# Moving the feed-forward evacuation of ScalarE, VectorE and GpSimd one piece later, behind the next attention step

## The chip, the core and the metric

The kernel runs on one core of a Trainium2 chip. The core has five engines that run side by side, each through its own list of instructions in order, and wait for one another by semaphores: TensorE (PE: matmuls; its weight loads are PEld), VectorE (DVE), ScalarE (ACT), GpSimd (POOL) and SyncE (SP, which here only starts DMAs). The metric is the device time of one execution in microseconds, lower is better. The chip grants TensorE one of two clocks, 1.2 or 2.4 GHz; the profile shows it as 0.50 and 1.00.

## The reference

Input x is 8 sequences of 512 tokens of 256 features, all float32. Four blocks are applied, each on a layernorm of x and added to x:

```python
x = x + ssm(layernorm(x))       # projection, rotary state space scan of 8 heads, gate, rms norm, projection
x = x + ffn(layernorm(x))
x = x + deltanet(layernorm(x))  # q, k, v, beta; delta-rule scan of 8 heads of 32; layernorm
x = x + ffn(layernorm(x))       # the same weights as above

def ffn(x):                     # ternary weights w, a scale s for each output feature
    h = silu(x @ w1.T * w1_s) * (x @ w2.T * w2_s)      # 256 -> 1024
    h = gelu(h @ h1.T * h1_s)                          # 1024 -> 1024
    h = gelu(h @ h2.T * h2_s)                          # 1024 -> 1024
    return h @ w3.T * w3_s                             # 1024 -> 256
```

## The kernel before, in words

A **stage** is the work of one attention block on one sequence: the state space block (`ssm_stage`, four tiles of 128 tokens, eight steps each) or the delta rule (`delta_stage`, 89 steps: 20 of projections and Gram matrices, 31 of a triangular inverse on VectorE, then the recurrence in blocks of 32 tokens). Beside each stage but the very first state space one, `window` runs the feed-forward block of another sequence (`ffn`). So there are 7 state space windows and 8 delta-rule windows, and one feed-forward block alone at the end.

The feed-forward block works on two units of 256 tokens. A unit is 18 **slices**, numbered s: 8 for w1/w2 (called w0 to w7 here, 8 matmuls each), 4 for h1 (h1.0 to h1.3, 32 matmuls), 4 for h2, one for the transposes of the next unit's input (xt) and one for w3 (32 matmuls). Each float32 operand is split in a high and a low part, so that matmuls come in pairs with `_hi` and `_lo`. A slice writes one of four PSUM banks, in a ring: `bank` makes slice s wait until slice s-4 has been read.

What the other engines do for a slice is its **evacuation**. For w slices: silu on ScalarE into `gate` (L698), the product on VectorE into `hid` (L899, which frees the bank, L902), the high part on VectorE (L903), the low part on GpSimd (L580). For h slices: two gelus on ScalarE (L702, L703), the high part (L706), the low part on GpSimd (L580). `hid` and `gate` have two buffers, so ScalarE's slice n waits for the low part of slice n-2 (L695). For w3: scale and residual on VectorE (L922, L925).

The order on every engine is written by the same function. A list (`SSM_PLAN`, `DELTA_PLAN`, made by `spread`) gives each attention step a number of slices; `window` (L129) emits attention step i, then all feed-forward pieces whose position lies below the sum of the plan up to i. A w slice and xt are one piece at position s; an h slice and w3 are two, at s and s + 0.5: for an h slice the first piece is 12 matmuls (input tiles k = 0 to 5 for the first half of the outputs), the second the other 20, of which the last 8 use k = 6 and 7. Each piece of TensorE waits for the low parts that it reads: slice h1.0 reads w0 to w7 (k = 0 to 7), and slice h2.0 reads h1.3 in its last 8 matmuls (L1215). The evacuation stands at s + 0.5, so it is emitted in the attention step in which TensorE's last piece of the slice is.

In a state space window a unit spans two tiles (a pair). TensorE's order around the places that matter is, for the first tile: projections (L1261), w1 to w5; cumulative sums (L1269 to L1281), w6, w7, h1.0 and 12 matmuls of h1.1; transposes L1290. For the second tile: transposes L1251, the end of h1.3; projections (L1261), h2.0; sums (L1269 to L1281), h2.1, h2.2; transposes L1290. ScalarE's part behind L1261 is softplus, two copies, silu and a copy (L722 to L730), for which it waits for VectorE's L942, which waits for L1261. VectorE's part behind the sums is a chain of 15 operations from L952 to L976, with sine and cosine on ScalarE in between.

## Time and profile before

| | |
|---|---|
| median of 3 runs | 3181.72 us (3176.04 to 3186.53) |
| the profiled execution | 3179.42 us, its span 3177.4 us, mean granted clock 0.891 |
| busy share of the span | PE 78%, PEld 69%, DVE 47%, ACT 36%, POOL 29% |
| chain that ended last, by engine | PE 46%, DVE 25%, ACT 10%, issue 10%, POOL 5%, DMA 3% |

The time of the runs and of the profiled execution differ by 2.3 us in the median. TensorE is the busiest engine, but it is idle for 686 us of the span, and a part of its busy time runs at the lower clock. So what counts is what TensorE waits for at each place of the order, and at which clock it goes on.

### The profile page before, as it was taken

To read this page: it belongs to the slowest core of one execution; us is meant where nothing else is said; L and a number is where in the kernel's file an instruction comes from. 1 tells how busy PE (TensorE), PEld (TensorE's weight loads), DVE (VectorE), ACT (ScalarE), POOL (GpSimd) and SP (SyncE) were. 2 spreads that over 40 slices of the span, in tenths; PEclk is the share of its full clock that TensorE was granted. 3 is DMA by queue.
4 is the path that set the end of the run, shared out by engine and by line. 5 is a ranking of instruction groups with operands and counts; after the bars stand their busy time and mean duration, and the time that the engine had idled before them with its cause. 6 is when DMAs were issued, how large, how long until landed. Compare 5 with 4: busy or idle time off the path is not lost.

```text
span 3177.4 us, 54420 instructions
## 1 busy us (share of the span) xinstructions
PE 2491.4 (78%) x20928; PEld 2195.7 (69%) x20928; DVE 1483.2 (47%) x3604; ACT 1157.8 (36%) x2426; POOL 926.0 (29%) x1216
## 2 busy tenths in 40 slices
PE   4678868888688886888868888678877888777688
PEld 3567757777577775787657776568766777666578
DVE  3434553445534445444454444545444444544541
ACT  2235432445225442245412544134432354323223
POOL 2123323233223232233323223232322233233233
PEclk7679988999799997999979998789987999898799
DMA  6000000000000000000000000000000000000000
GB/s 202 1 1 1 3 12 15 1 1 18 19 7 1 1 18 21 4 1 1 20 21 3 1 8 21 14 1 1 15 14 14 1 1 10 12 15 6 21 10 7
DMA packets 86976, 43.33 MB, mean 14 GB/s; under 512 B 71472, under 2 KB 81584, under 8 KB 86704
## 3 DMA queue, kind: packets, MB, share of 16 engines
q1 hardware_dynamic: 83040, 28.12, 3.5%
q0 software_dynamic: 3664, 11.53, 1.1%
q8 instruction: 177, 2.90, 0.4%
q14 instruction: 95, 0.78, 0.1%
HBM read 27.05 MB, written 12.58 MB: 12 GB/s over the span
## 4 chain that ended last, share of the span: by engine, by line
PE 46%; DVE 25%; ACT 10%; issue 10%; POOL 5%; DMA 3%; SPq 1%; DVEq 0%; POOLq 0%; ACTq 0%
PE F L1218 21%; DVE prod L1079 4%; DVE ti L1081 3%; PE Q L1261 3%; PE F L1240 2%; PE Q L1329 2%; PE Q L1346 2%; PE Q L1308 2%; POOL hA_lo L580 2%; DVE hid L899 2%; PE Q L1444 2%; PE Q L1414 1%; PE Q L1381 1%; PE Q L1300 1%; PE Q L1312 1%
## 5 line engine op out<-in xcount | busy, mean ns | idle before, releaser
L1218 PE MATMUL F<-hA_hi,h_sb 128*128 128x256 f32 x2048 | 568.1, 311 | 107.8 <-POOL hA_lo L580 107.4
L580 POOL TENSOR_TENSOR hA_lo<-hid,hA_hi 128x256 fp32r<-128x256 f32 (+1 forms) x384 | 353.0, 920 | 879.2 <-ACT hA_hi L706 494.0
L1218 PE MATMUL F<-hA_lo,h_sb 128*128 128x256 f32 x2048 | 542.9, 299 | 0.0
L1218 PE MATMUL F<-hB_hi,h_sb 128*128 128x256 f32 x2048 | 526.1, 295 | 0.3
L1218 PEld LDWEIGHTS F<-hA_hi,h_sb 128*128 128x128 f32 x2048 | 426.6, 208 | 127.9 <-POOL hA_lo L580 115.4
L1218 PE MATMUL F<-hB_lo,h_sb 128*128 128x256 f32 x2048 | 508.8, 287 | 0.0
L1198 PE MATMUL F<-xf_hi,w_sb 128*128 128x256 f32 x1024 | 319.0, 338 | 162.6 <-DVEq L902 69.2
L1218 PEld LDWEIGHTS F<-hA_lo,h_sb 128*128 128x128 f32 x2048 | 428.3, 209 | 0.5
L1218 PEld LDWEIGHTS F<-hB_hi,h_sb 128*128 128x128 f32 x2048 | 400.8, 196 | 19.0 <-issue 15.3
L1218 PEld LDWEIGHTS F<-hB_lo,h_sb 128*128 128x128 f32 x2048 | 401.7, 196 | 0.3
L1198 PEld LDWEIGHTS F<-xf_hi,w_sb 128*128 128x128 f32 x1024 | 234.9, 229 | 183.8 <-DVEq L902 82.9
L702 ACT ACTIVATE hid<-F,sh_sb 128x256 f32<-128x256 f32 x256 | 120.9, 472 | 558.0 <-PE F L1218 557.4
L580 POOL TENSOR_TENSOR hB_lo<-hid,hB_hi 128x512 fp32r<-128x512 f32 x128 | 163.9, 1280 | 525.6 <-ACT hB_hi L706 525.6
L1198 PE MATMUL F<-xf_lo,w_sb 128*128 128x256 f32 x1024 | 302.1, 322 | 0.0
L1198 PEld LDWEIGHTS F<-xf_lo,w_sb 128*128 128x128 f32 x1024 | 237.9, 232 | 0.3
L698 ACT ACTIVATE gate<-F,s_sb 128x256 f32<-128x256 f32 x256 | 116.2, 472 | 320.0 <-POOL hA_lo L580 255.8
L899 DVE SCALAR_TENSOR_TENSOR hid<-F,s_sb,gate 128x256 f32<-128x256 f32 x256 | 123.4, 482 | 199.0 <-ACT gate L698 147.0
L1079 DVE TENSOR_TENSOR prod<-ti,au 128x31 f32<-128x31 f32 (+15 forms) x248 | 117.5, 474 | 54.2 <-DMA au<-a_scr 46.1
L1261 PE MATMUL Q<-win_sb,xT 128*128 128x512 f32 (+1 forms) x384 | 139.3, 514 | 1.9 <-ACT xT L716 1.9
L1240 PE MATMUL F<-w_sb,hA_hi 128*128 128x256 f32 x512 | 129.2, 292 | 12.8 <-POOL hA_lo L580 12.8
L1240 PE MATMUL F<-w_sb,hA_lo 128*128 128x256 f32 x512 | 124.4, 282 | 0.0
L703 ACT ACTIVATE hid<-F,sh_sb 128x256 f32<-128x256 f32 x256 | 119.3, 466 | 0.0
(212 smaller groups left out, 4492.7 us busy)
## 6 DMA issues: line engine op xcount, KB each, us to landing
h_sb<-h_dram POOLq DMA_DIRECT2D x2, 4096.0 KB, 24.5
x_sb<-x_dram SPq DMA_DIRECT2D x8, 512.0 KB, 3.9
a_scr<-q_sb SPq DMA_DIRECT2D x128, 32.0 KB, 1.7
au<-a_scr SPq DMA_DIRECT2D x8, 512.0 KB, 3.2
t_scr<-ti SPq DMA_DIRECT2D x8, 512.0 KB, 3.0
tbd<-t_scr SPq DMA_DIRECT2D x128, 32.0 KB, 1.9
out_dram<-x_sb SPq DMA_DIRECT2D x8, 512.0 KB, 3.3
w_sb<-w_dram POOLq DMA_DIRECT2D x3, 1024.0 KB, 9.0
```

The costliest lines, as they stand in the source:

```text
L580: pool.tensor_tensor(lo, hid[:, n % 2, 0:w, :], hi.bitcast(F32), ALU.subtract).then_inc(f_lo.handle, 1)
L698: act.activation(gate[:, n % 2, :], ps[:, 0:TOK], ACT.Silu, scale=s1_sb[:, j:j + 1]).then_inc(f_act.handle, 1)
L702: act.activation(hid[:, n % 2, 0, :], ps[:, 0:TOK], ACT.Gelu, scale=scales[:, k:k + 1])
L703: own(act.activation(hid[:, n % 2, 1, :], ps[:, TOK:2 * TOK], ACT.Gelu, scale=scales[:, k + 1:k + 2]))
L899: own(dve.scalar_tensor_tensor(hid[:, n % 2, 0, :], bank_of(s)[:, TOK:2 * TOK], s2_sb[:, j:j + 1], gate[:, n % 2, :], ALU.mult, ALU.mult))
L1079: own(dve.tensor_tensor(pr, bcast(ti[:, 0:j + 1, j], 2, below), bcast(au[:, j + 1:BLK, j], 1, j + 1), ALU.mult))
L1081: own(dve.tensor_tensor(rest, rest, pr, ALU.subtract))
L1198: last = pe.matmul(ps[:, i * TOK:(i + 1) * TOK].rearrange("p (t n) -> p t n", t=2), w[:, k, j * P:(j + 1) * P], part[:, :, k, :], start=(k ...
L1218: last = pe.matmul(ps[:, i * TOK:(i + 1) * TOK], w[:, k, o:o + P], part[:, k, :], start=(i == 0 and k == 0 and part is src[0]), stop=(i == ...
L1240: last = pe.matmul(ps[:, t * D:(t + 1) * D], part[:, k, t * P:(t + 1) * P], w3_sb[:, k, :], start=(k == 0 and part is hA_hi), stop=(k == K ...
L1261: last = pe.matmul(Q[q][:, 0:c1 - c0], xT[:, k, :], win_sb[:, k, c0:c1], start=(k == 0), stop=(k == 1))
L1308: pe.matmul(Q[3][:, h * HP:(h + 1) * HP], seg[:, h, :], xdt[:, h, :], start=True, stop=True)
```

## The change

The evacuation of every slice moves from position s + 0.5 to s + 1 on ScalarE, VectorE and GpSimd (`TAIL`). It is then emitted in the step in which TensorE's first piece of the next slice is, behind that step's attention work. Where a plan step holds several slices, only the last one's evacuation moves to a later step. `window` gets a last call that emits what is left. TensorE's order is the same as before, and so is that of the DMAs.

```diff
--- before.py
+++ after.py
@@ -52,6 +52,7 @@
 SUB0 = D1_STEPS * NT
 D20 = SUB0 + SUB_STEPS + 2
 U_AHEAD, WT_AHEAD = 3, 5
+TAIL = 1.0
 
 
 def spread(shares):
@@ -135,6 +136,7 @@
         att.before(step + 1)
         done += slices
         mlp.before(done)
+    mlp.before(done + 1)
 
 
 def alone(stage):
@@ -569,7 +571,7 @@
             def ffn(p, b, final):
                 for u in range(UNITS):
                     for j in range(HSLICES):
-                        yield u * SLICES + j + 0.5
+                        yield u * SLICES + j + TAIL
                         n = u * HSLICES + j
 
                         if j < KT:
@@ -579,7 +581,7 @@
                         hi, lo, w = ffn_dst(j)
                         pool.tensor_tensor(lo, hid[:, n % 2, 0:w, :], hi.bitcast(F32),
                                            ALU.subtract).then_inc(f_lo.handle, 1)
-                    yield u * SLICES + W3_SLICE + 0.5
+                    yield u * SLICES + W3_SLICE + TAIL
                     if not final:
                         rsqrt_delta(b, u)
 
@@ -689,7 +691,7 @@
                     for j in range(HSLICES):
                         n = u * HSLICES + j
                         s = s0 + j
-                        yield s + 0.5
+                        yield s + TAIL
 
                         act.wait_ge(f_ps.handle, f_ps.at(p, s + 1))
                         act.wait_ge(f_lo.handle, f_lo.at(p, n - 1))
@@ -704,7 +706,7 @@
                                            scale=scales[:, k + 1:k + 2]))
                         act.sem_inc(f_freeA.handle, 1)
                         act.copy(ffn_dst(j)[0], hid[:, n % 2]).then_inc(f_hiA.handle, 1)
-                    yield s0 + XT_SLICE + 0.5
+                    yield s0 + XT_SLICE + TAIL
                     if u + 1 < UNITS or more:
                         xt_high(p, s0 + XT_SLICE)
 
@@ -891,7 +893,7 @@
                     for j in range(HSLICES):
                         n = u * HSLICES + j
                         s = s0 + j
-                        yield s + 0.5
+                        yield s + TAIL
                         if j < KT:
 
                             dve.wait_ge(f_act.handle, f_act.at(p, u * KT + j + 1))
@@ -907,7 +909,7 @@
                             elif b_next is not None:
                                 norm_unit(p + 1, x_slot(b_next), 0)
                     s = s0 + XT_SLICE
-                    yield s + 0.5
+                    yield s + TAIL
                     if u + 1 < UNITS:
                         xt_low(p, s, p, u + 1)
                     elif b_next is not None:
@@ -915,7 +917,7 @@
                     else:
                         dve.sem_inc(f_freeV.handle, 1)
                     s = s0 + W3_SLICE
-                    yield s + 0.5
+                    yield s + TAIL
 
                     dve.wait_ge(f_ps.handle, f_ps.at(p, s + 1))
                     o = bank_of(s)[:].rearrange("p (t d) -> p t d", t=2)
```

**ScalarE, second tile of a pair in a state space window.** Before, from the transposed input's copy (L716) on; F0 holds slice h1.3, Q1 to Q3 hold the projections:

```order
L716 COPY xT<-Q0 128x256
L702 ACTIVATE hid<-F0,sh1_sb 128x256
L703 ACTIVATE hid<-F0,sh1_sb 128x256
L706 CAST hB_hi<-hid 128x512
L719 ACT_TABLE_LOAD
L722 ACTIVATE dtab<-dtv 128x8
L723 ACTIVATE dte<-dtab 128x8
L724 ACTIVATE dtl<-dte 128x8
L725 COPY bc<-Q3 128x128
L726 COPY xs<-Q2 128x512
L727 ACT_TABLE_LOAD
L727 ACTIVATE sz<-Q1 128x512
```

The same place now (line numbers are higher by two); the rows that follow are the second gelu and the high part `hB_hi` of h1.3:

```order
L718 COPY xT<-Q0 128x256
L721 ACT_TABLE_LOAD
L724 ACTIVATE dtab<-dtv 128x8
L725 ACTIVATE dte<-dtab 128x8
L726 ACTIVATE dtl<-dte 128x8
L727 COPY bc<-Q3 128x128
L728 COPY xs<-Q2 128x512
L729 ACT_TABLE_LOAD
L729 ACTIVATE sz<-Q1 128x512
L732 COPY hat<-bc 128x16x32
L704 ACT_TABLE_LOAD
L704 ACTIVATE hid<-F0,sh1_sb 128x256
```

The evacuation of h1.3 (two gelus and `hB_hi`) stood ahead of softplus, the copies and silu of the projections; now it stands behind them and behind a table load. GpSimd's low part of h1.3 (L580) waits for that `hB_hi`.

**VectorE, first tile of a pair in a state space window.** Before, between `seg` of the attention step and `sums` of the next; F2, F3, F0, F1, F2 hold w1 to w5:

```order
L947 TENSOR_TENSOR seg<-stri,dta 128x1024
L899 SCALAR_TENSOR_TENSOR hid<-F2,s2_sb,gate 128x256
L903 CAST hA_hi<-hid 128x256
L899 SCALAR_TENSOR_TENSOR hid<-F3,s2_sb,gate 128x256
L903 CAST hA_hi<-hid 128x256
L899 SCALAR_TENSOR_TENSOR hid<-F0,s2_sb,gate 128x256
L903 CAST hA_hi<-hid 128x256
L899 SCALAR_TENSOR_TENSOR hid<-F1,s2_sb,gate 128x256
L903 CAST hA_hi<-hid 128x256
L899 SCALAR_TENSOR_TENSOR hid<-F2,s2_sb,gate 128x256
L903 CAST hA_hi<-hid 128x256
L952 COPY sums<-Q0 128x40
```

Now:

```order
L949 TENSOR_TENSOR seg<-stri,dta 128x1024
L901 SCALAR_TENSOR_TENSOR hid<-F1,s2_sb,gate 128x256
L905 CAST hA_hi<-hid 128x256
L901 SCALAR_TENSOR_TENSOR hid<-F2,s2_sb,gate 128x256
L905 CAST hA_hi<-hid 128x256
L901 SCALAR_TENSOR_TENSOR hid<-F3,s2_sb,gate 128x256
L905 CAST hA_hi<-hid 128x256
L901 SCALAR_TENSOR_TENSOR hid<-F0,s2_sb,gate 128x256
L905 CAST hA_hi<-hid 128x256
L901 SCALAR_TENSOR_TENSOR hid<-F1,s2_sb,gate 128x256
L905 CAST hA_hi<-hid 128x256
L954 COPY sums<-Q0 128x40
```

The five evacuations in this gap are now those of w0 to w4 (F1, F2, F3, F0, F1); that of w5 stands behind the chain that `sums` begins, together with w6 and w7.

**VectorE, end of the triangular inverse in a delta-rule window.** Before, around the last two steps of the inverse (L1079, L1081); F1 and F2 hold w2 and w3 of the second unit; a row without a tile's name only computes or waits:

```order
L1079 TENSOR_TENSOR prod<-ti,au 128x60
L1081 TENSOR_TENSOR ti<-ti,prod 128x30x2
L897 REGISTER_ALU
L898 REGISTER_ALU
L899 SCALAR_TENSOR_TENSOR hid<-F1,s2_sb,gate 128x256
L903 CAST hA_hi<-hid 128x256
L1079 TENSOR_TENSOR prod<-ti,au 128x31
L1081 TENSOR_TENSOR ti<-ti,prod 128x31
L897 REGISTER_ALU
L898 REGISTER_ALU
L899 SCALAR_TENSOR_TENSOR hid<-F2,s2_sb,gate 128x256
L903 CAST hA_hi<-hid 128x256
```

Now, where F0 and F1 hold w1 and w2:

```order
L1081 TENSOR_TENSOR prod<-ti,au 128x60
L1083 TENSOR_TENSOR ti<-ti,prod 128x30x2
L899 REGISTER_ALU
L900 REGISTER_ALU
L901 SCALAR_TENSOR_TENSOR hid<-F0,s2_sb,gate 128x256
L905 CAST hA_hi<-hid 128x256
L1081 TENSOR_TENSOR prod<-ti,au 128x31
L1083 TENSOR_TENSOR ti<-ti,prod 128x31
L899 REGISTER_ALU
L900 REGISTER_ALU
L901 SCALAR_TENSOR_TENSOR hid<-F1,s2_sb,gate 128x256
L905 CAST hA_hi<-hid 128x256
```

One evacuation fewer (that of w2) stands ahead of the last step of the inverse.

## Rows read from the trace of the kernel before

**Rows 1.** page, part 5: line, engine, output <- inputs, count, busy, mean, idle before
```profile
L1218 PE MATMUL F<-hA_hi,h_sb 128*128 128x256 f32 x2048 | 568.1, 311 | 107.8 <-POOL hA_lo L580 107.4
...
L1218 PE MATMUL F<-hB_hi,h_sb 128*128 128x256 f32 x2048 | 526.1, 295 | 0.3
```

**Rows 2.** waits over the span: waiter, its releaser, us in total, times, longest
```profile
PE F L1218 <- POOL hA_lo L580: 107.4, 32, 8.3
PE F L1198 <- DVEq L902: 69.2, 40, 4.2
...
PE Q L1367 <- ACT kqpad L766: 21.3, 30, 1.2
```

**Rows 3.** one line each: durations ns, first and last start us, form and count
```profile
L589 POOL MEMSET hst<- x8: 301/311/311, 19.8 to 2498.6; 128x256 f32 x8
...
L615 POOL MEMSET kqpad<- x8: 952/954/955, 366.9 to 2879.6; 128x1024 f32 x8
```

**Rows 4.** timeline of ScalarE, second tile of a pair, start and length in us
```profile
1778.91 0.62 ACT L706 CAST hB_hi<-hid 128x512 fp32r<-128x512 f32 x1
...
1785.32 0.62 ACT L730 COPY hat<-bc 128x512 f32<-128x512 f32 x1
1785.96 1.28 ACT L702 ACT_TABLE_LOAD   x1
...
1788.20 0.62 ACT L706 CAST hA_hi<-hid 128x512 fp32r<-128x512 f32 x1
```

**Rows 5.** timeline of GpSimd over the same stretch
```profile
1779.60 1.26 POOL L580 TENSOR_TENSOR hB_lo<-hid,hB_hi 128x512 fp32r<-128x512 f32 x1 [5.55 <-ACT hB_hi L706]
1788.90 1.30 POOL L580 TENSOR_TENSOR hA_lo<-hid,hA_hi 128x512 fp32r<-128x512 f32 x1 [8.04 <-ACT hA_hi L706]
```

**Rows 6.** timeline of TensorE over the same stretch
```profile
1781.49 0.37 PE L1218 MATMUL F<-hB_hi,h_sb 128*128 128x256 f32 x1
...
1784.45 0.28 PE L1218 MATMUL F<-hB_hi,h_sb 128*128 128x256 f32 x1
...
1785.41 0.29 PE L1269 MATMUL Q<-dta,tri 128*128 128x16 f32 x2
```

**Rows 7.** timeline of TensorE in the first tile of the pair
```profile
1735.78 0.39 PE L1198 MATMUL F<-xf_hi,w_sb 128*128 128x256 f32 x1 [1.47 <-DVEq L902]
...
1743.18 0.28 PE L1218 MATMUL F<-hA_hi,h_sb 128*128 128x256 f32 x1
...
1752.85 0.58 PE L1218 MATMUL F<-hA_hi,h_sb 128*128 128x256 f32 x1 [6.63 <-POOL hA_lo L580]
```

**Rows 8.** timeline of GpSimd in the first tile of the pair
```profile
1752.07 0.72 POOL L580 TENSOR_TENSOR hA_lo<-hid,hA_hi 128x256 fp32r<-128x256 f32 x1 [2.26 <-DVE hA_hi L903]
1753.02 0.73 POOL L580 TENSOR_TENSOR hA_lo<-hid,hA_hi 128x256 fp32r<-128x256 f32 x1 [0.23 <-DVE hA_hi L903]
```

**Rows 9.** window, length, busy of PE, PEld, DVE, ACT, POOL, granted clock, DMA, GB/s
```profile
1727.20:1906.60 179.40, 151.99 (x1195) 138.77 (x1194) 83.29 (x178) 86.87 (x160) 52.00 (x63) 0.94 0.01 4
1752.80:1758.00 5.20, 5.00 (x21) 4.70 (x22) 0.14 (x1) 2.32 (x4) 0.73 (x1) 0.50 0.00 0
1758.00:1761.40 3.40, 3.40 (x31) 3.27 (x29) 0.69 (x1) 1.01 (x2) 1.29 (x1) 0.99 0.00 0
```

**Rows 10.** timeline of VectorE in a delta-rule stage
```profile
1975.98 0.74 DVE L858 TENSOR_SCALAR xnf<-x_sb,fmv,frstd 128x256 f32 x2 [0.43 <-DVE pc L1068]
...
2016.92 0.49 DVE L899 SCALAR_TENSOR_TENSOR hid<-F,s_sb,gate 128x256 f32<-128x256 f32 x1 [0.21 <-DVE ti L1081]
...
2017.76 0.20 DVE L1079 TENSOR_TENSOR prod<-ti,au 128x31 f32<-128x31 f32 x1
```

**Rows 11.** timeline of TensorE, end of the triangular inverse
```profile
2024.85 0.44 PE L1381 MATMUL Q<-tbd,uw 128*32 128x128 f32 x4 [5.25 <-DMA tbd<-t_scr]
```

**Rows 12.** timeline of ScalarE just after it
```profile
2028.90 0.47 ACT L698 ACTIVATE gate<-F,s_sb 128x256 f32<-128x256 f32 x1 [1.41 <-PE F L1198]
```

## The prediction

> **What bounds the kernel now.** I read four views in this order: the costliest groups of the page, the list of waits, the timelines of one state space window and one delta-rule window, and busy time by window. In the page, TensorE is the busiest engine; the reader is to see where it is idle ahead of a matmul. The h1 slices (they read hA) are idle for 107.8 us in all, nearly all of it behind GpSimd's low parts [rows 1]; that is the step from w7 to h1.0, 32 waits of up to 8.3 us [rows 2]. The h2 slices (they read hB) are idle for 0.3 us [rows 1]: at the step from h1.3 to h2.0 nothing waits today. The w slices wait 69.2 us for a bank that VectorE has not read yet [rows 2]. So the evacuation of w slices already has no slack, and that of h slices has some. The question is whether the slack holds where the evacuation is moved, and what the attention chain gains by going first.
>
> TensorE's order is unchanged, and what it emits after a wait comes later by the whole wait. A state space window lasts 179.4 us with TensorE busy for 152.0 at a mean clock of 0.94 [rows 9], so a new wait of TensorE there is paid nearly in full. There are 8 state space stages, the first without a feed-forward block, and 8 delta-rule stages, counted by their first memsets [rows 3]. That makes 7 state space windows with two units each, 14 pairs of tiles, and 8 delta-rule windows. All rows from 1735 to 1791 us are of one such pair; the others repeat it.
>
> **Part 1: h1.3 behind softplus and silu, in the second tile of each pair.** Before, ScalarE writes the high part of h1.3 at 1778.91 [rows 4] and GpSimd's low part is done at 1779.60 + 1.26 = 1780.86 [rows 5], before TensorE starts h2.0 at 1781.49 [rows 6]. Now this evacuation stands behind ScalarE's part of the projections, whose last instruction (L730) starts at 1785.32 [rows 4]. Nothing makes that part earlier: it waits for matmuls of TensorE that stand where they stood. Right behind L730 the trace shows how long an evacuation takes there, since today that is the place of the one of h2.0: table load at 1785.96, high part at 1788.20 [rows 4], low part at 1788.90 + 1.30 = 1790.20 [rows 5]. The low part of h1.3 will be there at this time. TensorE's h2.0 can do 24 of its 32 matmuls without it, until 1784.45 [rows 6]; that is 24 in 2.96 us, or 0.123 us each. Then it waits until about 1790.25: **5.8 us**. Behind it on TensorE stand 8 matmuls, then the sums (L1269, at 1785.41 today [rows 6]) on which VectorE's chain for this tile begins. So attention and feed-forward both come 5.8 us later, and no other work of TensorE covers it.
>
> Afterwards the clock is low. After the wait of 6.63 us in the first tile [rows 7] the granted clock is 0.50 for 5.20 us, in which 21 matmuls are recorded (0.248 us each), and then 0.99 [rows 9]. I take the same after the new wait: half of 5.20 is 2.6 us. Sum 8.4 us per pair. The bounds are 5.8 (the clock stays up) and 11.0 (a low stretch twice as long).
>
> One rule bears on this length. The Trainium skill, "ScalarE: Activation LUTs", What ACT_TABLE_LOAD costs, says that each switch to another table set costs a drain of about 1.38 us on top of the 1.28 us load. Here the load ahead of the gelus lasts 1.28 us and starts 0.02 us after L730 ends [rows 4], with no drain to be seen; the trace decides. By the page the wait would be an estimated 1.4 us longer, or 20 us in all.
>
> **Part 2: w0 to w4 instead of w1 to w5, in the first tile.** The evacuations between the projections and the sums stay five. TensorE stalls for a bank at w5 today (it resumes at 1735.78 after 1.47 us [rows 7]); now it stalls at w4, since w4 needs the bank of w0. It resumes at the same time and is one slice of 8 matmuls, 1.0 us, later. That 1.0 us costs nothing: it lies ahead of the wait of 6.63 us, and VectorE reaches the sums after five evacuations, as before.
>
> What costs is that w5 is now evacuated behind VectorE's chain, with w6 and w7. Before, TensorE did the 24 matmuls of h1.0 that use k = 0 to 5 from 1743.18 on, at full speed, and then waited until 1752.85 [rows 7] for the low part of w6, done at 1752.07 + 0.72 [rows 8]. Now that is the time at which the low part of w5 is done, and only the 10 matmuls with k = 0 to 4 go ahead of the wait. The low part of w6 follows at 1753.75 as that of w7 does now [rows 8]. That of w7 needs, from 1752.79 on, when the low part of w5 frees its buffer, a silu of 0.47 us [rows 12], a product and high part of 0.84 [rows 10], a low part of 0.73 [rows 8] and some 0.3 between them: 1755.15, 1.4 us later than now. TensorE has 14 matmuls to do until then. So 14 matmuls move from before the wait to behind it, into the low clock. Behind the wait stand 34 instead of 20 up to the next attention step: 21 in the 5.2 us of low clock, 13 at 0.123. **1.6 us** per pair. Bounds: 1.4 (only the lateness of w7) and 3.5 (all 14 at 0.248).
>
> **Part 3: the rest of a state space window.** h1.0 to h1.2, h2.0 to h2.3 and xt change places with attention work that is done by then, or find the same neighbours; their low parts are read one layer later. ScalarE saves one table load per pair, since w0 is evacuated with w1, in a place where ScalarE waits for VectorE anyway. w3's VectorE work goes behind the tile's residual; it reaches the output store on SP's queue later, but still ahead of the next stage's stores. I cost all this at nothing; if the cover were gone, it would be one table load of 1.28 us [rows 4] per pair, either way.
>
> **Part 4: the delta-rule windows.** Four small terms.
> - w2's two VectorE operations leave the path to the end of the inverse: the stretch from L899 at 2016.92 to the next L1079 at 2017.76, with the 0.21 us of idle ahead [rows 10]: -1.0 us. TensorE waits 5.25 us for the DMAs behind that end [rows 11], so the gain arrives. TensorE's w slices come later in the inverse, and must then be done before 2024.85; today the wait of 5.25 us is their room.
> - The input norm for the next unit (`xnf`, 0.74 us) stands today in VectorE's wait for a DMA and goes in between steps of the inverse [rows 10]: +0.7 us.
> - ScalarE's copy of u after the inverse no longer stands behind the silu of w7 (0.47 us, 0.4 without the overlap [rows 12]): -0.4 us.
> - In the projections, the pads (L1367 waits 21.3 us in all for ScalarE's [rows 2], 2.7 per window) come a little earlier behind h and w slices, and once later behind h2.1: I take -0.5 us; the bounds are -2.7 and +0.7, the last being one more evacuation's remainder.
>
> Sum -1.2 us per window, bounds -3.4 (the pads at their lower end) and +1.0 (the pads at their upper end, and the gain of w2 lost in the DMAs' wait).
>
> **The sum.** 14 x (8.4 + 1.6) = +140; 8 x (-1.2) = -10; together +130 us. The profiled execution took 3179.4 us, so 3309; it lies 2.3 us below the median of the runs, so against the median 3312.
>
> **Rivals.**
> - *The clock stays up.* Only the waits count: 14 x (5.8 + 1.4) = +101, with -10: about 3273. For it: the new wait of 5.8 is shorter than the 6.63 us after which the rows show the low clock. Against it: the difference is small, and the low stretch in [rows 9] is long.
> - *The banks run dry.* Where the order of freeing shifts (w4 on w0, and w3 to w6 in the inverse), TensorE's 69.2 us of bank waits [rows 2] could double in place of hiding in later waits: +69 on top, 3381. Against it: each of these places has a longer wait of TensorE close behind it.
> - *The evacuation of h1.3 hides, and the attention chain gains.* This is the other side. If TensorE's last 8 matmuls of h2.0 did not have to wait (low parts ready before 1784.45), only the gains stay: -10 from part 4, and up to one table load per pair on ScalarE, 14 x 1.28 = 18. Then 3154 to 3172. It decides at 1784.45: ScalarE would have to be through L730 and the evacuation 5.8 us earlier than the rows say [rows 4 to 6]. Nothing in the profile shows how.
> - *The change does nothing.* If the moved pieces had been idle time on all engines, the time would be that of before, 3182. The idle 0.3 us ahead of hB [rows 1] speaks for slack today; the order shows that the slack is used up.
>
> **Chances and range.** Forecast 0.78, clock stays up 0.10, banks 0.05, the other side 0.05, nothing 0.02. A measurement of this kernel tells about 0.3%, or 10 us, from no change. Faster by more: 0.05. Within: 0.02. Slower by more: 0.93. The forecast's own ends are 14 x (5.8 + 1.4) - 27 = +74 and 14 x (11.0 + 3.5) + 8 = +211; neither is likely to come with all terms at once. The range takes in the clock rival below and half of the way to the upper end: 3255 to 3350.
>
> **What would show it.** In the profile after: a wait of L1218 on hB for GpSimd's hB_lo of about 5.8 us, 14 times, some 80 us in all, where it is 0.3 now. The wait for hA_lo longer by about 1 us each and starting earlier, at k = 5. State space windows of about 199 us instead of 179.4, delta-rule windows unchanged within 2 us. ScalarE's table loads fewer by 14. A mean granted clock a little under 0.891. I am wrong if hB waits stay near zero, if the delta-rule windows grow, or if the state space windows grow by more than 25 us.

## The result and the profile after

The changed kernel takes 3300.77 us (median of 3 runs, 3300.73 to 3304.43), the kernel before 3181.72: a ratio of 1.0377, with a 95% interval of 1.0363 to 1.0391, so 119 us slower. The profiled execution of after has a span of 3299.0 us (before 3177.4) and a mean granted clock of 0.880 (0.891). Line numbers of after are 1 or 2 higher than those of before. Of all timings one is left out below: a run of the kernel with only the w slices put back took 7690 us at a mean clock of 0.321, while its other three took 3296 to 3306.

The costliest groups of after that answer to [rows 1]; the last two numbers are idle time ahead and what ended it:

```profile
L1220 PE MATMUL F<-hA_hi,h_sb 128*128 128x256 f32 x2048 | 565.3, 310 | 126.4 <-POOL hA_lo L582 126.3
L1220 PE MATMUL F<-hB_hi,h_sb 128*128 128x256 f32 x2048 | 540.7, 301 | 79.8 <-POOL hB_lo L582 78.7
```

And TensorE's waits, as in [rows 2] (total us, times, longest):

```profile
PE F L1220 <- POOL hA_lo L582: 126.3, 18, 9.4
PE F L1220 <- POOL hB_lo L582: 78.7, 16, 5.6
PE F L1200 <- DVEq L904: 63.8, 40, 2.7
```

The h2 slices waited 0.3 us before and wait 79.8 now: that is the new wait of 5.6 us, 14 times. The wait ahead of h1.0 has grown from 107.4 to 126.3 in all and its longest from 8.3 to 9.4. The bank waits of the w slices did not grow (69.2 before).

The windows that answer to [rows 9], a state space one and a delta-rule one (length, busy time by engine, granted clock):

```profile
1801.30:1999.40 198.10, 156.82 (x1190) 144.18 (x1193) 82.18 (x178) 84.25 (x159) 53.11 (x64) 0.90 0.00 1
1999.40:2203.80 204.40, 158.03 (x1426) 135.22 (x1426) 103.09 (x273) 58.12 (x144) 62.00 (x86) 0.88 0.07 17
```

Windows are measured from one memset of a stage to the next [rows 3]. The mean of the 7 state space windows rose from 180.6 to 199.7 us, that is +134 in all; the mean of the first 7 delta-rule windows fell from 205.2 to 204.1, and the last one with what follows it from 297.7 to 294.0: some -11 in all.

**The new wait.** ScalarE, GpSimd and TensorE in the second tile of a pair, after; they answer to [rows 4 to 6]:

```profile
1860.87 0.62 ACT L732 COPY hat<-bc 128x512 f32<-128x512 f32 x1
1861.51 1.28 ACT L704 ACT_TABLE_LOAD   x1
1862.80 0.47 ACT L704 ACTIVATE hid<-F,sh_sb 128x256 f32<-128x256 f32 x1
1863.75 0.62 ACT L708 CAST hB_hi<-hid 128x512 fp32r<-128x512 f32 x1
```

```profile
1864.45 1.26 POOL L582 TENSOR_TENSOR hB_lo<-hid,hB_hi 128x512 fp32r<-128x512 f32 x1 [14.85 <-ACT hB_hi L708]
```

```profile
1859.88 0.28 PE L1220 MATMUL F<-hB_lo,h_sb 128*128 128x256 f32 x1
1865.76 0.58 PE L1220 MATMUL F<-hB_hi,h_sb 128*128 128x256 f32 x1 [5.60 <-POOL hB_lo L582]
1867.43 0.41 PE L1220 MATMUL F<-hB_lo,h_sb 128*128 128x256 f32 x1
1867.64 0.44 PE L1271 MATMUL Q<-dta,tri 128*128 128x16 f32 x2
```

TensorE does its 24 matmuls from 1857.04 to 1860.16 and stands until the low part lands. ScalarE starts the evacuation only behind L732, and the table load ahead of it takes its 1.28 us and nothing more: the gelu starts 0.01 us behind its end. The 8 matmuls behind the wait are 0.21 us apart, not 0.12: the clock is low. Granted clock around the wait (TensorE's busy time is the second number of a row, the clock the third from the end):

```profile
1860.00:1862.00 2.00, 0.16 (x2) 0.00 (x0) 0.00 (x0) 1.86 (x4) 0.00 (x0) 1.00 0.00 0
1862.00:1864.00 2.00, 0.00 (x0) 0.00 (x0) 0.00 (x0) 1.88 (x4) 0.00 (x0) 0.67 0.00 0
1864.00:1866.00 2.00, 0.24 (x1) 0.24 (x2) 0.00 (x0) 0.37 (x1) 1.26 (x1) 0.50 0.00 0
1870.00:1872.00 2.00, 2.00 (x11) 1.85 (x10) 1.94 (x2) 0.00 (x0) 1.82 (x2) 0.50 0.00 0
1872.00:1876.00 4.00, 4.00 (x32) 4.00 (x32) 1.74 (x6) 2.44 (x5) 0.00 (x0) 0.88 0.00 0
```

It falls inside the wait and is back at 1.00 only in the stretch from 1872 on, some 7 us after TensorE went on at 1865.76. It does so in all 14 pairs.

**The longer wait in the first tile**, the place of [rows 7]. The first row is the last matmul with k = 4:

```profile
1817.63 0.28 PE L1220 MATMUL F<-hA_lo,h_sb 128*128 128x256 f32 x1
1827.26 0.58 PE L1220 MATMUL F<-hA_hi,h_sb 128*128 128x256 f32 x1 [9.35 <-POOL hA_lo L582]
```

Ten matmuls go ahead of it (24 before), and it lasts 9.35 us. The 6.63 us of [rows 7] are not the right measure for it. In that pair the clock was low ahead of h1.0, TensorE was 1.6 us late there, and the wait was that much shorter. In 7 of the 14 pairs of before, with the clock at 1.00 there, it lasted 8.1 to 8.3 us; this is one of them:

```profile
1842.14 0.58 PE L1218 MATMUL F<-hA_hi,h_sb 128*128 128x256 f32 x1 [8.28 <-POOL hA_lo L580]
```

Counted from the projections, the wait ends 0.3 us later than before in the first pair of a window and at the same time in the second (27.7 against 27.4 us, and 26.4 in both). What costs is behind it: from there to the transposes L1290 it takes 6.3 and 6.7 us in place of 5.0 and 4.9.

**What came back.** In the second tile of before, ScalarE evacuates h2.1 and h2.2 ahead of its copy bT (the second matrix that the scores are made of), and the scores (L1300) wait. ScalarE, then TensorE, of the kernel before:

```profile
1798.78 0.62 ACT L706 CAST hA_hi<-hid 128x512 fp32r<-128x512 f32 x1
1799.31 0.58 ACT L750 COPY bT<-Q 128x512 f32<-128x512 f32 x1
```

```profile
1799.94 1.16 PE L1300 MATMUL Q<-cT,bT 64*128 64x128 f32 x16 [1.59 <-ACT bT L750]
```

After, TensorE reaches the scores without a wait:

```profile
1883.14 1.16 PE L1302 MATMUL Q<-cT,bT 64*128 64x128 f32 x16
```

This is not because ScalarE is earlier. h2.2's evacuation now stands behind bT, but that of h2.0 has moved into the place ahead of it, so two still go first, and bT starts 14.9 us behind the sums (13.9 before):

```profile
1882.51 0.58 ACT L752 COPY bT<-Q 128x512 f32<-128x512 f32 x1
```

TensorE, slowed by the low clock, is 2.8 us later at the transposes and so comes to the scores when bT is there.

In a table, stretches of TensorE's order, medians of the windows from the second on, in us, to about 0.1. In the first tile only the sum of the two rows counts: TensorE comes to the sums one slice later, and the long wait behind them takes most of that up.

| tile, from ... to | before | after | difference |
|---|---|---|---|
| first: projections to sums | 10.84 | 11.78 | +0.9 |
| first: sums to transposes L1290 | 20.92 | 21.72 | +0.8 |
| second: projections to sums | 7.73 | 14.41 | +6.7 |
| second: sums to transposes | 10.47 | 13.24 | +2.8 |
| second: transposes to those of y | 15.47 | 13.84 | -1.6 |

With the small rest that is 9.4 us per pair. The first window has grown more, by 21.5 us in all; with it the 14 pairs give the 134 us.

### The profile page after: what moved, and what is told of

Same layout as the page of the kernel before. It is cut to its first block, busy times and chain, and to the rows that moved or that the text cites. A ratio compares the mean times of both kernels' runs of the same rounds, so it can differ in the third digit from the quotient of the medians.

```text
span 3299.0 us, 54384 instructions
## 1 busy us (share of the span) xinstructions
PE 2537.1 (77%) x20897; PEld 2242.8 (68%) x20928; DVE 1483.4 (45%) x3604; ACT 1135.1 (34%) x2412; POOL 932.6 (28%) x1216
## 4 chain that ended last, share of the span: by engine, by line
PE 46%; DVE 21%; issue 16%; POOL 6%; ACT 5%; DMA 3%; SPq 1%; DVEq 0%; POOLq 0%; ACTq 0%
PE F L1220 21%; DVE prod L1081 3%; DVE ti L1083 3%; PE Q L1348 3%; PE F L1242 2%; PE Q L1310 2%; PE F L1200 2%; POOL hB_lo L582 2%; POOL hA_lo L582 2%; PE Q L1446 1%; PE Q L1283 1%; PE Q L1331 1%; POOL rn L626 1%; PE Q L1383 1%; PE Q L1302 1%
## 5 line engine op out<-in xcount | busy, mean ns | idle before, releaser
L1220 PE MATMUL F<-hA_hi,h_sb 128*128 128x256 f32 x2048 | 565.3, 310 | 126.4 <-POOL hA_lo L582 126.3
L1220 PE MATMUL F<-hB_hi,h_sb 128*128 128x256 f32 x2048 | 540.7, 301 | 79.8 <-POOL hB_lo L582 78.7
L1220 PE MATMUL F<-hB_lo,h_sb 128*128 128x256 f32 x2048 | 518.6, 290 | 0.0
L1220 PEld LDWEIGHTS F<-hB_hi,h_sb 128*128 128x128 f32 x2048 | 409.8, 200 | 104.5 <-POOL hB_lo L582 84.7
L1200 PE MATMUL F<-xf_hi,w_sb 128*128 128x256 f32 x1024 | 326.1, 344 | 156.0 <-DVEq L904 63.8
L1220 PEld LDWEIGHTS F<-hB_lo,h_sb 128*128 128x128 f32 x2048 | 409.6, 200 | 0.3
L1081 DVE TENSOR_TENSOR prod<-ti,au 128x31 f32<-128x31 f32 (+15 forms) x248 | 115.1, 464 | 61.2 <-DMA au<-a_scr 53.1
L1242 PE MATMUL F<-w_sb,hA_hi 128*128 128x256 f32 x512 | 136.9, 303 | 2.7 <-POOL hA_lo L582 2.7
L1242 PE MATMUL F<-w_sb,hA_lo 128*128 128x256 f32 x512 | 131.9, 294 | 0.0
```

Source lines behind the costliest of these rows:

```text
L1081: own(dve.tensor_tensor(pr, bcast(ti[:, 0:j + 1, j], 2, below), bcast(au[:, j + 1:BLK, j], 1, j + 1), ALU.mult))
L1200: last = pe.matmul(ps[:, i * TOK:(i + 1) * TOK].rearrange("p (t n) -> p t n", t=2), w[:, k, j * P:(j + 1) * P], part[:, :, k, :], start=(k ...
L1220: last = pe.matmul(ps[:, i * TOK:(i + 1) * TOK], w[:, k, o:o + P], part[:, k, :], start=(i == 0 and k == 0 and part is src[0]), stop=(i == ...
L1242: last = pe.matmul(ps[:, t * D:(t + 1) * D], part[:, k, t * P:(t + 1) * P], w3_sb[:, k, :], start=(k == 0 and part is hA_hi), stop=(k == K ...
```

## The experiments

Each was timed on the chip beside the kernel before; the ratio is to that kernel's runs in the same series. In the short diffs `tail(j)` is the distance at which the evacuation of slice j stands: 0.5 is before, 1.0 is after. KT is 8, so j = KT + 3 is h1.3, KT + 5 is h2.1, KT + 6 is h2.2; `ssm` is true in state space windows. The lines that call `tail` on the three engines and pass `ssm` and `fill` on are left out.

### One slice put back, or moved alone

**Only h1.3 put back.**

```diff
-TAIL = 1.0
+def tail(j):
+    return 0.5 if j == KT + 3 else 1.0
```

> Only the evacuation of h1.3 goes back to its old place (position s + 0.5); all others stay one piece later. Theory (the h1.3 step carries 9.2 us per pair of tiles, of which 1.6 is given back when the copy of bT no longer stalls TensorE): 14 x 7.6 = 106 us less than the changed kernel, 3190 to 3200; what is left over the kernel before is 14 x 1.7 for w5 minus 1.5 per delta-rule window, about +12. Rival (the loss is spread over many moved evacuations and bank waits): less than half goes back, 3240 or more.

Measured 3168.31 us, ratio 0.9955 (0.9938 to 0.9971). One slice carries the whole loss, 4.2% or 134 us between this and the changed kernel. It went further than expected: the kernel without it is faster than before.

**Only the w slices put back.**

```diff
-TAIL = 1.0
+def tail(j):
+    return 0.5 if j < KT else 1.0
```

> Only the evacuations of the w slices go back to their old place. Theory: the first tile of each pair gets its 1.7 us back (14 x 1.7 = 23), the delta-rule windows lose the 1.0 us that w2 gave the inverse and about 0.7 at the pads (8 x 1.5 = 12): about 3290, at most 20 us below the changed kernel's 3301. The wait of h1 slices for hA_lo returns from 126 to about 107 us. Rival (bank waits of the w slices are the main loss): 3240 or less.

Measured 3298.46 us (median of three), ratio 1.0374 (1.0350 to 1.0399): no change. The state space windows gained (199.7 to 197.0 on average), but the delta-rule windows lost (204.1 to 205.4, and 2.5 at the end). So the w slices cost 2.7 us in a state space window, 1.4 per pair and 19 in all, and bring some 12 of it back in the delta rule.

**Before, with only h1.3 late.**

```diff
+def tail(j):
+    return 1.0 if j == KT + 3 else 0.5
```

> The kernel before with one edit: only the evacuation of h1.3 stands one piece later. Theory: this alone gives a wait of TensorE for hB_lo of 5.6 us, 14 times (79 us in all), and 14 x 7.6 = 106 us of time: about 3288. Rival (it takes several moved evacuations together): 3240 or less.

Measured 3294.24 us, ratio 1.0346 (1.0328 to 1.0364). Its one moved slice makes the same wait on hB (78.8 us in all) and a state space window of 198.5 us, +18.0. That is 9.0 per pair for h1.3 alone.

### The clock and the stall for bT, two by two

**Fillers in the new wait.** 40 matmuls go ahead of the first wait for k = 6 of h2.0, into a bank that the next slice overwrites; nobody reads them.

```diff
+                                if ks.start and layer == 1 and j == 0 and fill:
+                                    spare = bank(p, s + 1)
+                                    for m in range(fill):
+                                        pe.matmul(spare[:, 0:TOK], w[:, m % 6, 0:P], src[0][:, m % 6, :],
+                                                  start=True, stop=True, skip_group_check=True)
```

> The changed kernel with 40 more matmuls of 256 columns on TensorE in each state space unit, between the 24th matmul of h2.0 and the wait for h1.3's low part; they write the free bank of h2.1 and nothing reads them. They add 40 x 0.123 = 4.9 us of work into a wait of 5.6 us and keep TensorE busy. Theory (of the 9.2 us per pair, 5.6 is the wait and 3.4 is the low clock behind it): the granted clock stays at 1.00 behind the wait, and 3.4 us per pair come back less up to 1.6 of a returning stall on bT: 14 x 1.8 to 14 x 3.4, so 25 to 48 us less than the changed kernel, 3253 to 3276. Rival (the clock does not matter, all is waiting): no change, 3301 within 5, or slower by the added work.

Measured 3285.51 us, ratio 1.0316 (1.0295 to 1.0337). By the ratios that is 19 us less than the changed kernel where 25 to 48 were expected. Behind the wait that is left, 0.8 us, the clock stays at 1.00 in all 14 pairs, and the two stretches of the second tile are 13.61 and 10.47 (after: 14.41 and 13.24): 3.6 us won. But the next one, transposes to y, takes 17.41 in nine pairs and 15.91 in five, in place of 13.84. So of the three together next to nothing is won in the nine and 1.5 us in the five. A part of the 19 us lies elsewhere: the first seven delta-rule windows are 1.3 us shorter each (202.8 against 204.1). The waits show where the rest went (fillers, TensorE):

```profile
PE Q L1307 <- ACT bT L752: 28.3, 14, 2.0
...
PE F L1225 <- POOL hB_lo L582: 11.7, 16, 0.8
```

The stall for bT is back, 2.0 us in every pair. TensorE is 3.6 us earlier at the transposes, ScalarE at bT only 1.4, with its two evacuations (h2.0 and h2.1) ahead. That stall explains the 15.91. In the nine other pairs the clock falls behind it and costs 1.5 us more, as here, where the scores start at 1873.83 (length, TensorE busy, clock):

```profile
1874.00:1876.00 2.00, 2.00 (x21) 1.88 (x22) 0.96 (x2) 1.13 (x3) 1.32 (x2) 0.77 0.00 0
1876.00:1878.00 2.00, 2.00 (x12) 2.00 (x11) 0.32 (x1) 0.00 (x0) 0.61 (x1) 0.50 0.00 0
```

To test the part of bT, h2.1 is moved behind bT, without and with the fillers:

```diff
-TAIL = 1.0
+tail = lambda j, ssm: (2.0 if j == KT + 5 else 1.0) if ssm else 1.0
```

> Changed kernel with ScalarE's evacuation of h2.1 in the state space windows one piece later still, behind bT, and no fillers. Theory (without fillers the stretch from the sums to the transposes is 13.2 us, and bT is no longer what TensorE waits for, so its neighbour does not matter; the gain of that move with fillers, 0.8% of the time, is there only because the clock was kept up): 0 to -6 us against the changed kernel, ratio 1.035 to 1.038. Rival (the two edits are independent): -25 us, ratio 1.030.

Without fillers: 3304.84 us, ratio 1.0392 (1.0376 to 1.0409). No gain; the stretch to y is 13.83, as without the move.

> Changed kernel with the 40 filler matmuls in TensorE's wait for the low part of h1.3 (as in the run with fillers, 1.0316 of before), and ScalarE's evacuation of h2.1 in the state space windows one piece later still, behind bT. Theory (the fillers keep the clock up, and 2 us of the 2.8 us gained so were lost again in the stall for bT behind two evacuations): the stall of 2.02 us goes, 14 x -1.9 = -27 us against the run with fillers alone, 3256 us, ratio 1.023 to 1.026. Rival (the time was not held by bT but by VectorE's chain and the low parts behind it): ratio 1.030 to 1.033, with a wait of the same length elsewhere.

With fillers: 3250.08 us, ratio 1.0238 (1.0223 to 1.0254), and the stall of 2.0 is down to 0.6:

```profile
PE Q L1307 <- ACT bT L752: 7.7, 14, 0.6
```

The three stretches are now 13.61, 10.47 and 14.44, that is 3.0 us less. The clock stays at 1.00 through all three stretches in all pairs. So keeping the clock up behind the new wait is worth about 3.0 us per pair, and it can be had in full only if bT no longer stands behind two evacuations. By the ratios the fillers alone give 19 us, the move alone nothing, the two together 44.

### The parts that gain

**Before, with h2.2 alone late, in state space windows.**

```diff
+tail = lambda j, ssm: (1.0 if j == KT + 6 else 0.5) if ssm else 0.5
```

> Kernel before, with one single evacuation moved: that of h2.2 in the state space windows, from ahead of ScalarE's copy bT to behind it (VectorE's xnf goes behind cT too). Theory (TensorE's stall of 1.59 us for bT in the second tile is what the change gave back, and it can be had without the wait for h1.3): the stall goes, h2.3 and w3 have room enough, 14 x -1.4 = -20 us, 3162 us, ratio 0.994; the stretch from the transposes to y in second tiles falls from 15.5 to about 13.9 us. Rival (the gain is hidden by the next thing that waits: the low part of h2.2 or the bank for w3, late): 0 to -5 us, ratio 0.998 to 1.000, with a new wait of TensorE on hA or on a bank behind the transposes.

Measured 3155.6 us, ratio 0.9939 (0.9925 to 0.9953): -19 us, as expected. Before, the line of waits `PE Q L1300 <- ACT bT L750` held 22.3 us in 14 waits; here it is gone, and transposes to y takes 14.0 in place of 15.5. One evacuation stands ahead of bT here, not two, and TensorE is not late: so this gain is not the same as the one seen in after, where TensorE's lateness covers the copy.

**Only the delta-rule windows late; then only their w slices.**

```diff
+tail = lambda j, ssm: 0.5 if ssm else 1.0
```

> Kernel before, with the evacuation moved (s + 1) in the 8 delta-rule windows alone; state space windows as before. Theory (from the run with h1.3 alone put back, 0.9955 of before: the delta-rule windows gain 1.6 us each and more): 8 x -1.6 = -13 us, 3169 us, ratio 0.996; state space windows 179.4 us each; delta-rule windows about 204.6 against 206.3. Rival (the gain in that run came from the state space windows, a table load or the stall at bT): no change, ratio 1.000. Second rival (the delta-rule windows lose when their neighbours do not move): over 1.002.

Measured 3151.3 us, ratio 0.9931 (0.9918 to 0.9944): -22 us, more than expected.

```diff
+tail = lambda j, ssm: 0.5 if ssm else (1.0 if j < KT else 0.5)
```

> Kernel before, with only the w slices' evacuation moved (s + 1), in the delta-rule windows alone; h slices, xt and w3 as before. Theory (the terms of the prediction: w2 out of the way to the inverse's end -1.0, u's copy ahead of a silu -0.4 per window; the rest of what the full delta-rule move gives, 22 us, comes from the h slices between the projections and pads): 8 x -1.4 = -11 us, ratio 0.9965. Rival (nearly all of the 22 us comes from the w slices): ratio 0.993 to 0.994. Rival (the inverse's end is hidden by the DMAs behind it): 0.999 to 1.000.

Measured 3155.91 us, ratio 0.9923 (0.9909 to 0.9938): -24 us, the rival. The w slices alone give as much as all slices do; with all of them late the stretch up to the inverse is 2.0 us shorter still, but the norm takes its 1.0 back in the inverse and the recurrence, by its clock, most of the rest. A delta-rule window is 3.2 us shorter on average. Of that 1.4 lie in the inverse, from its first VectorE operation to the memset behind it (36.1 to 34.7). w2's two operations and the idle ahead are 1.0 of it. The other 0.4 is one long sum fewer. Each low part that GpSimd makes at the end of the inverse lengthens the sum beside it: three before (w0, w1, w2: 0.74, 0.72 and 0.72 us), two in this run, and the sum that stood beside w0's has its short length. VectorE of before, then of this run, then GpSimd of before (w0's low part):

```profile
2011.95 0.74 DVE L1081 TENSOR_TENSOR ti<-ti,prod 128x156 f32<-128x156 f32 x1
```

```profile
1997.26 0.32 DVE L1083 TENSOR_TENSOR ti<-ti,prod 128x156 f32<-128x156 f32 x1
```

```profile
2011.64 0.86 POOL L580 TENSOR_TENSOR hA_lo<-hid,hA_hi 128x256 fp32r<-128x256 f32 x1 [3.37 <-DVE hA_hi L903]
```

Of the rest, 1.2 us lie behind the inverse, in the recurrence, and there it is clock: its third tile has the same matmuls in both kernels, but takes 18.6 us in five of the first seven windows before and in one here, and 17.2 in the others. Before, then this run (length, TensorE busy, clock):

```profile
2064.20:2082.80 18.60, 16.65 (x212) 0.91 0.01 2
```

```profile
2048.20:2065.40 17.20, 15.24 (x213) 1.00 0.01 2
```

Why the clock is granted in one and not in the other is open: TensorE's waits of over 0.6 us inside the recurrence are the same in both.

Why then do these windows gain only 1.1 us on average in the changed kernel? Its recurrence is 1.8 us faster than before (the third tile takes 17.2 in every window) and its inverse 0.4, but up to the inverse it is 1.1 us slower. It begins the delta-rule window in a low clock that the state space window leaves behind. The first 4 us of such a window before, after, and with only the delta rule late (length, TensorE busy, clock):

```profile
1906.60:1910.60 4.00, 4.00 (x23) 1.00 0.41 137
```

```profile
1999.40:2003.40 4.00, 4.00 (x18) 0.59 0.40 135
```

```profile
1892.50:1896.50 4.00, 4.00 (x23) 1.00 0.41 135
```

The first tile of that window then takes 20.3 us, with only the delta rule late 18.2. But a low start does not by itself make a window longer. With h2.2 alone late, six of the first seven delta-rule windows start at 0.57. Their first tile takes 19.4 us (18.8 before), and the seven last 204.2 us on average against 205.2 before: other tiles find a full clock instead. So the low start is what the rows show, and that it alone holds the changed kernel back is argued, not shown.

### A version that beats both, and what fillers add

**h2.2 late in state space windows; in delta-rule windows all late but h1.3 and h2.2.**

```diff
-TAIL = 1.0
+tail = lambda j, ssm: (1.0 if j == KT + 6 else 0.5) if ssm else (0.5 if j in (KT + 3, KT + 6) else 1.0)
```

> State space windows as in the run with h2.2 alone moved; delta-rule windows as in the changed kernel, but the evacuations of h1.3 and h2.2 left at s + 0.5 there (so that the next unit's input norm stays in VectorE's wait for a DMA, 0.7 us). Theory: the terms add: -20 (bT) - 13 (delta rule) - 5 (norm) = 3144 us, ratio 0.988. Rival (the norm costs nothing where it stands, or h2.2 at s + 0.5 costs as much elsewhere): -33 us, 3149, ratio 0.9895. Rival (the bT gain is hidden): 3163 to 3167.

Measured 3134.13 us, ratio 0.9873 (0.9857 to 0.9889). The two parts add (-19 and -22, measured apart), and the norm at its old place brings nothing that can be seen in the time, though the inverse is shorter by 1.0 us than in the run with only the delta rule late.

**46 fillers ahead of the wait for w6 in h1.0 on top; then h1.0's evacuation behind bT too.**

```diff
+                                            if layer == 0 and k == KT - 2 and fill:
+                                                spare = bank(p, s + 1)
+                                                for m in range(fill):
...
-tail = lambda j, ssm: (1.0 if j == KT + 6 else 0.5) if ssm else ...
+tail = lambda j, ssm: (1.0 if j == KT + 6 else 1.5 if j == KT else 0.5) if ssm else ...
```

> The best kernel so far (0.9873 of before) with 46 filler matmuls, whose sums nobody reads, ahead of TensorE's wait for the low part of w6 in h1.0 (6.6 us, first tile of each pair, state space windows). Theory (the clock is at 0.50 behind this wait for 5.2 us because TensorE stood still; kept busy, it stays up, 2.6 us are saved, and some 0.7 of them are lost at ScalarE's bT behind the evacuation of h1.0): 14 x -1.9 = -27 us, 3107 us, ratio 0.979. Rival (TensorE is not what holds the first tile there; all of it comes back as a stall for bT, 1.9 us): -10 us or less, ratio 0.984 to 0.987. Rival (the fillers run over the wait's end and delay): over 0.987.

> As the run with 46 fillers, and ScalarE's evacuation of h1.0 in the state space windows moved behind bT as well (with the table load ahead of it, 1.28 us). Theory (bT then follows the transposes at once): 14 x -0.7 = -10 us further, 3097 us, ratio 0.976. Rival (bT was not waited for; VectorE's cT holds the same place): no difference from the run before. Rival (h1.1 and h1.2 find their buffer late and the low part of h1.0 to h1.3 is late for h2.0): slower than the run before.

Measured 3125.67 us, ratio 0.9833 (0.9815 to 0.9852), and 3128.07 us, 0.9840 (0.9824 to 0.9856). The first is the fastest kernel of this study, but the gain over the version without fillers is 13 us where 27 were expected; the second move adds nothing that the intervals can tell. TensorE's waits on hA without and with fillers:

```profile
PE F L1220 <- POOL hA_lo L582: 115.7, 32, 8.3
```

```profile
PE F L1225 <- POOL hA_lo L582: 36.1, 32, 2.8
```

80 us of waiting are gone from the list and 13 from the time: idle time filled with useless work is no gain by itself, and the clock was not held. 46 fillers were worked out for a wait of 6.6 us, but in 12 of the 14 pairs of the kernel without them it is 8.1 to 8.3 us. So TensorE still stood for 2.6 to 2.8 us behind the fillers in nine pairs, and for 0.9 to 1.1 in five. The clock fell in 11 of the 14; in the one shown, TensorE had stood for 1.12 and 0.45 us (length, TensorE busy, clock):

```profile
1719.30:1721.30 2.00, 1.55 (x9) 0.75 0.00 0
1721.30:1723.30 2.00, 2.00 (x12) 0.50 0.00 0
1723.30:1725.30 2.00, 2.00 (x17) 0.89 0.00 0
```

The low stretch is shorter, not gone.

## Why the prediction was right, and where its terms were not

- **The wait for h1.3.** Forecast 5.8 us, 14 times, some 80 us; measured 5.60 and 78.7. The method worked: put the moved evacuation where the trace shows its neighbour today, and see how far TensorE gets without it.
- **The low clock behind it.** Forecast 2.6; measured 3.0 (what the two edits together won back) to 3.9 (the stretches of the second tile: 6.7 and 2.8, less the wait of 5.6). The low stretch was taken as the 5.2 us of the first tile and lasted some 7. The rival in which the clock stays up is out: it fell behind a wait of 5.6 us as behind one of 6.63.
- **w5.** Forecast +1.6 per pair; measured +1.7 in the first tile and 1.4 per pair by putting the w slices back. As forecast, TensorE's late arrival at the sums costs next to nothing and the matmuls behind the wait are the loss. By the prediction's own terms they are +1.8: 5.2 + 1.6 for the 34, against 4.96 for the 20 of [rows 7]. The bank waits did not double; that rival is out too.
- **"I cost all this at nothing"** (part 3) was the step that failed. It left out TensorE's stall for bT, `PE Q L1300 <- ACT bT L750` with 22.3 us in 14 waits in the list of waits of before. The prediction adds the wait and the low clock in full, as if TensorE met the same stall behind them. It does not: it is late, bT is there, and 1.6 us per pair, some 20 us in all, are absorbed. What shows that it is lateness is the run with fillers: with the clock up and the same order on ScalarE the stall is back, and longer, 2.0 us. The order alone gives about half: with only h1.3 put back and the clock at 1.00, transposes to y takes 14.6 us in place of 15.5. So moved slices can meet new neighbours on the path of the attention step, as h2.0 and h2.2 did at bT.
- **The delta rule.** Forecast -1.2 per window, measured -1.1 on average, but not by its terms. Taking w2 out of the inverse was mis-sized, -1.0 against -1.4, by the 0.4 of the sum beside GpSimd's part; the norm put into it costs 1.0 (35.6 with it, 34.6 without) and not 0.7. So the inverse gave -0.4 where the two terms give -0.3. ScalarE's copy of u (-0.4) gave nothing: TensorE is at the transposes of u 3.74 us after L1381 in six of seven windows before, and as late in six of seven with only the w slices late. TensorE's waits for the pads fell from 52.5 to 42.8 us in all (31.2 for VectorE's and 21.3 for ScalarE's before, 24.5 and 18.3 after), or 1.2 per window where 0.5 was taken, but what of that reaches a window's end cannot be told from the clock. The clock was not foreseen at all: the recurrence gained 1.8 us, by clock as far as its third tile shows, and the first tile of the window lost 1.6 (20.4 against 18.8), with the low clock at its start. That the sum came out right is luck.
- **The sum.** 14 x 10.0 - 10 = +130 forecast; 134 - 11 and about -1 elsewhere in the profiled execution, +119 between the medians. The forecast of the sum missed by less than its parts did: h1.3 was 1 us too cheap per pair and the 1.6 us that the stall for bT absorbs were missing. These two nearly cancel, and that is luck.

## What to carry to other kernels

Work that is moved one place later in an engine's order is priced by two lists: who reads its result (here TensorE, for h1.3), and who stood behind it until now (here bT, behind h2.2). Both must be read in the new order, with every moved piece in its new place: h2.2 left its place ahead of bT, and h2.0 came into it. The first list gave the loss of 134 us, single moves that clear the way for what stood behind gave 19 us and, with the help of the clock, 22, and slice by slice the good half could be kept without the bad one. A low clock behind a wait is worth money only if the engine that comes next is not late anyway; check by removing both.

## What the runs showed of the hardware

**A VectorE operation beside a GpSimd one.** VectorE and GpSimd at the start of the inverse, with only the delta rule late:

```profile
1967.66 0.25 DVE L1083 TENSOR_TENSOR ti<-ti,prod 128x87 f32<-128x87 f32 x1
1967.94 0.35 DVE L1081 TENSOR_TENSOR prod<-ti,au 128x112 f32<-128x112 f32 x1
1968.32 1.22 DVE L1083 TENSOR_TENSOR ti<-ti,prod 128x112 f32<-128x112 f32 x1
```

```profile
1968.14 1.28 POOL L582 TENSOR_TENSOR hA_lo<-hid,hA_hi 128x512 fp32r<-128x512 f32 x1 [2.53 <-ACT hA_hi L708]
```

The sum of 128x112 lasts 1.22 us where the one of 128x87 lasts 0.25; it ends at 1969.54, 0.12 behind GpSimd's end at 1969.42. In the changed kernel the same happens to the norm, VectorE then GpSimd:

```profile
2079.26 1.75 DVE L860 TENSOR_SCALAR xnf<-x_sb,fmv,frstd 128x256 f32 x2 [0.33 <-DVE ti L1083]
```

```profile
2079.61 1.26 POOL L582 TENSOR_TENSOR hA_lo<-hid,hA_hi 128x512 fp32r<-128x512 f32 x1 [2.87 <-ACT hA_hi L708]
```

1.75 us for the two, where they take 0.74 alone [rows 10]. So a low part on GpSimd can cost VectorE up to 1 us, by when it falls; the 0.4 us in the inverse above is the same thing. The Trainium skill, "SBUF — State Buffer", SBUF: two separate sides, says that the two engines share a pair of ports under an exclusive lock: for VectorE operations in a two-port mode or with two SBUF inputs, the engine that starts first has the pair for its whole instruction, and the other blocks fully. The rows agree: the sum, which starts 0.18 us behind GpSimd's operation, and the second part of the norm, which starts with it, end 0.12 and 0.14 us behind its end.

**The clock.** It fell after TensorE had stood for 5.60 us, in all 14 pairs (after). It stayed at 1.00 in all 14 behind 40 fillers and a gap of 0.8 us, and in all 14 behind the stall of 1.59 us for bT (before). Behind the stall of 2.0 us in the run with 40 fillers it fell in 9 pairs of 14. With 46 fillers it fell in 11 of 14, one of them behind gaps of 1.12 and 0.45 us, and stayed up in three, one of them behind a gap of 2.77 us. So the length of the last gap alone does not decide it, and what does is open. A state space window can hand a low clock to the window behind it: the first tile there took 20.3 us against 18.2 in one kernel and 19.4 against 18.8 in another.
